# Value rows of the first batch: fetched by GpSimd's indirect DMAs instead of SyncE's loads

## The reference, cut to what matters

```python
query_sparse = relu(einsum('btd,nde->btne', x, enc_q))
value_sparse = relu(einsum('btd,nde->btne', x, enc_v))
idx, mask = _causal_window_indices(Tt, WINDOW)             # 64 rows back
dist = sqrt((diff * diff * m_h).sum(-1) + 1e-08)           # diff = key - query
neg_d, loc = top_k(-dist, 32)
infl = exp(-topd) / (exp(-topd).sum(-1) + 1e-08)
context = einsum('btk,btkd->btd', infl, v_h[batch_ix, top_idx])
out = (q_h * (context + gate * 0.1 * heb_ctx)) @ decoder
```

## Time and profile before

| | |
|---|---|
| median of 2 runs | 807.11 us (805.77 to 808.45) |
| the profiled execution's own time | 806.9 us, span 805.1 us |
| busy, share of the span | PE 88%, DVE 84%, POOL 53%, ACT 52% |
| busy share of the 16 DMA engines | 8.9% on SP's queue |
| mean granted clock of TensorE | 0.926 of full speed |

### The profile page before, as it was taken

The page is one execution under the profiler, slowest core; times in us unless marked ns, Lnnn a source line. Parts: engine busy times, 40 slices in busy tenths (PEclk is TensorE's granted clock), DMA queues, the critical chain, the costliest instruction groups (busy, mean ns, idle before and its releaser), DMA issues.

```text
span 805.1 us, 11834 instructions
## 1 busy us (share of the span) xinstructions
PE 708.7 (88%) x3368; PEld 504.3 (63%) x3368; DVE 678.5 (84%) x2785; ACT 416.6 (52%) x754; POOL 424.4 (53%) x504
## 2 busy tenths in 40 slices
PE   3979998998997999998997999999998899888833
PEld 2636765665665676665575667676766676667823
DVE  3876768769989999979879989976799999758894
ACT  2745353654766465464556464456674455466300
POOL 2265355564657654564655846564747656434131
PEclk9978999999989999999999999999999999995555
DMA  9920000000000000001000000001000000010000
GB/s 290 347 61 1 1 0 0 2 1 19 12 1 10 10 14 7 14 2 30 15 1 10 9 7 17 11 1 32 13 1 10 8 16 17 3 41 6 18 26 18
DMA packets 25697, 22.17 MB, mean 28 GB/s; under 512 B 1892, under 2 KB 23424, under 8 KB 25120
## 3 DMA queue, kind: packets, MB, share of 16 engines
q1 hardware_dynamic: 25632, 21.40, 8.9%
HBM read 19.17 MB, written 2.23 MB: 27 GB/s over the span
## 4 chain that ended last, share of the span: by engine, by line
DVE 49%; PE 35%; issue 5%; ACT 5%; DMA 4%; POOL 1%; SPq 0%; DVEq 0%; ACTq 0%
DVE S L790 12%; PE bank_G L505 9%; PE bank_X L505 9%; DVE Wk L1192 8%; PE bank_U L505 8%; PE bank_A L505 8%; DVE m L1189 6%; DVE Wk L798 5%; DMA vw<-vscratch 4%; DVE GWk L790 2%; DVE Wlo L790 2%; ACT L1261 2%; ACT Ed L1256 1%; DVE wT L790 1%; DVE La L790 1%
## 5 line engine op out<-in xcount | busy, mean ns | idle before, releaser
L505 PE MATMUL bank_A<-S,WdT 128*128 128x512 f32 x368 | 189.3, 614 | 11.6 <-DVE S L790 8.1
L1498 POOL TENSOR_TENSOR Wlo<-Wgu,Whi 128x256 fp32r<-128x256 f32 x138 | 111.1, 811 | 132.3 <-ACT Whi L1256 131.8
L1256 ACT ACTIVATE S<-bank_G 128x512 f32<-128x512 f32 x184 | 108.1, 595 | 124.0 <-PE bank_G L505 106.1
L1498 POOL TENSOR_TENSOR S<-S,Rb 128x512 f32<-128x512 f32 x88 | 120.2, 1367 | 78.1 <-DVE S L790 74.6
L790 DVE TENSOR_TENSOR S<-S,bank_U 128x512 f32<-128x512 f32 x184 | 123.6, 678 | 40.5 <-PE bank_U L505 28.7
L1256 ACT ACTIVATE Whi<-Wgu 128x256 fp32r<-128x256 f32 x184 | 74.4, 413 | 79.8 <-PE bank_U L505 76.4
L505 PE MATMUL bank_U<-xH,Whi 128*128 128x512 f32 x184 | 97.7, 531 | 6.2 <-DVE S L790 6.2
L505 PE MATMUL bank_G<-xH,Whi 128*128 128x512 f32 x184 | 100.7, 547 | 1.7 <-POOL Wlo L1498 1.6
L505 PEld LDWEIGHTS bank_A<-S,WdT 128*128 128x128 f32 x368 | 67.1, 194 | 50.2 <-issue 21.8
L790 DVE TENSOR_TENSOR S<-S,Rb 128x512 f32<-128x512 f32 x88 | 84.3, 959 | 2.6 <-ACT Rb L1256 0.6
L1192 DVE MATCH_REPLACE8 Wk<-m,Wk 128x79 f32<-128x79 f32 x384 | 81.7, 222 | 0.0
(11 more groups left out here) (232 smaller groups left out, 1444.8 us busy)
## 6 DMA issues: line engine op xcount, KB each, us to landing
vw<-vscratch SPq DMA_DIRECT2D x32, 158.0 KB
Wgu<-in_Wgu SPq DMA_DIRECT2D x2, 2048.0 KB, 15.3
xs<-in_x SPq DMA_DIRECT2D x4, 256.0 KB, 7.0
wqk<-in_w_qkv SPq DMA_DIRECT2D x1, 1024.0 KB, 7.5
Wgu<-in_Wgu SPq DMA_DIRECT2D x1, 1024.0 KB, 9.3
vscratch<-mo SPq DMA_DIRECT2D x4, 256.0 KB
out<-xs SPq DMA_DIRECT2D x3, 256.0 KB, 2.3
Wgu<-in_Wgu SPq DMA_DIRECT2D x1, 512.0 KB, 5.5
```

The costliest lines, as they stand in the source:

```text
L505: return engine.matmul(dst, lhsT, rhs, start=start, stop=stop)
L1256: return engine.activation(dst, src, f, bias=bias, scale=scale, accum_out=acc)
L1498: return engine.tensor_tensor(dst, a, b, op)
```

## The change

Only batch 0 changes its way of fetching. GpSimd writes a table `row_of` of 128 x 32 row numbers once (partition `p`, column `n` holds `16 n + p`). For each of the 8 groups it issues four indirect DMAs of 79 rows, one per tile, 32 in all, each of which reads its row numbers from a column of the table. They wait for the same things as the loads did: the stored value rows, and `ctx` of group `g - 2`. SP no longer issues the 8 loads of batch 0, and PE waits for all four fetches of a group. The batches 1 to 3 keep SP's loads. The table `ORDER` is new for PE, DVE, ACT and POOL over the whole program; its SP string differs in one place. The bodies of all other steps are the same.

```diff
@@ ORDER @@
     "sp":
-        "vvvvvvvvvsvvvvvvvvvsvvvvvvvvvsvvvvvvvssvvss",
+        "vvvvvvvvvsvvvvvvvvvsvvvvvvvvvsvvvvvvsvsvvss",
...
@@ program
+        U32 = mybir.dt.uint32
+        row_of = sb("row_of", [128, NG * GT], U32)
@@ values() of sync_engine
                     for g in range(NG):
                         yield
+                        if b == 0:
+                            continue
                         if g == 0:
                             sp.wait_ge(f"st_v{b}", 32)
                         if g >= 2:
                             sp.wait_ge(full(bank("ctx", b, g - 2)), nth("ctx", b, g - 2) + 1)
-                        elif b > 0:
+                        else:
                             sp.wait_ge(full(bank("ctx", b - 1, g + NG - 2)), nth("ctx", b - 1, g + NG - 2) + 1)
                         load(f"ld_v{g % 2}", vw[g % 2][:, :, :], windows(b, g))
@@ turns() of tensor_engine
-                    pe.wait_ge(f"ld_v{s}", 16 * (b * (NG // 2) + g // 2 + 1))
+                    if b:
+                        pe.wait_ge(f"ld_v{s}", 16 * ((b - 1) * (NG // 2) + g // 2 + 1))
+                    else:
+                        pe.wait_ge(f"ld_i{s}", 16 * GT * (g // 2 + 1))
@@ gpsimd_engine
+            def fetches():
+
+                yield
+                engine.iota(row_of[:, :], [[TQ, NG * GT]], base=0, channel_multiplier=1).then_inc(sems("row_of"), 1)
+                rows = vd[0]
+                for g in range(NG):
+                    for i in range(GT):
+                        yield
+                        po.wait_ge("row_of", 1)
+                        po.wait_ge("st_v0", 32)
+                        if g >= 2:
+                            po.wait_ge(full(bank("ctx", 0, g - 2)), nth("ctx", 0, g - 2) + 1)
+                        n = GT * g + i
+                        engine.indirect_dma_start(vw[g % 2][:, i, :], None, rows,
+                                                  bass.IndirectOffsetOnAxis(row_of[0:WK, n:n + 1], 0)).then_inc(
+                                                      sems(f"ld_i{g % 2}"), 16)
@@
-                  q=every(weights), p=every(adds))
+                  q=every(weights), p=every(adds), v=fetches())
```

More of the change, by code:

```diff
@@ L38 @@
     "sp":
-        "vvvvvvvvvsvvvvvvvvvsvvvvvvvvvsvvvvvvvssvvss",
+        "vvvvvvvvvsvvvvvvvvvsvvvvvvvvvsvvvvvvsvsvvss",
     "pe":
[L41 to L48, removed]
+        "yyeeyeeemeeeemaeeaeeeeeeeayasammmsmmaeemaesemsmeeeeeemmeeeemeeumemeeeumaemameaeeemeeaeeemuemummeeeye"
@@ new lines @@
+        "emmmymeeeeeemeeymeemeeemmemeeemeeememeeeeemmmyemeseeseesemseemeemeeeemmemyeemymeeheemeyeeemmeemeemee"
+        "emeeemeeeheeeehhmmhhmehhemmmeeemyheeeeededamdmaedaeeadaetmdatmamdmteetmeeeeedmmeemeemteeeemeeateaeea"
+        "emamtmmtsetseefeeemmfteeemmteeemmteeefeeefmfmeeteetmfemefeemfmeemsmseeeyeeteytemmthyeetemmteeememmet"
+        "meheeheememeeeehhmheheyheemammheeeeemdmdmaedaeemedaedamteeedteaeeaeteedtmmemmdmeeemteemeeeetmetmemee"
+        "aeemteeataeeaeemesemsmfmetfeetfteefefmefmtemtemeefmefmetmetsetsemeteetememeeeaeeetmmeahmmeemeeeeemee"
@@ L49 @@
+        "mheehemheheehamhhmmmeeememheaeeeedmdedmaemdeeameemeedteatdmeemdmeemmetemteeedemeammeeetemtatemaeeemm"
+        "eeeaeetefteefmmmtmeeeeeeetemtmmemmfeeeeteemteemmeeeetmtmtmmfhtftffthfhfhhfhfhhfffhfdfdddttddddtttttt"
         "tttttttttttt",
     "dve":
-        "yyyyyyyylyyyeycyeyeyyyyeyayeyylyyycayeyyeyymlmmyeayemyyaeaemaeaemeluemauelemuueeuumauueulemeuaemelem"
-        "eemeyyyyyyyylemeyyyemyeyyemlyyyyeyemeyyelememyeyyyemleemeyyemleeeemlehhemhhelemhhyyeyemyyyyyyleyyyem"
-        "yeyhyyyyheymehyyemhhhlyooeemoeaoaemoklkkkoekaemkkakakolkoekakgkkemgaekemkkaeemklekgemkkkekgkleaemagy"
@@ L54 @@
[L54 to L58, removed]
@@ L59 @@
-    "act":
[L60 to L65, removed]
@@ L66 @@
-    "pool":
[L67 to L70, removed]
+        "yyyyyyyyylyyyeycyeyyeyyeyyyyaeylayeceyyyylyyymmamyeemyyaaeemaeaelmeuueuemeluauuumuuueemeaelmeaemeelm"
@@ new lines @@
+        "eemeelmeyyyyyeemyelymyyyyeyyyeymyyeyeylmyeyemeyyyeymleemeemylyeeeelmyyhyhehehymeyelmhyhyyyeyyeyeymye"
+        "lmeyyyeymeyylyhemhehhhheemyoleoemoemoaokakkkokkkaklkeoaeaokkkgkamkaekekmegkelmkekaeekmgelmkkkkakeeag"
+        "ymkeygkylkeemkegkmyekyelmefkgkeefmkkelmekgkfekmekkfeleemgeelmyygyhyhyhyhyyegyeymeyyhyhylyeymyeygyhye"
+        "ymeelmehhyhheemheomleoaooaemokkkeokekoamlkkkekegaoekkakkkmlgkkaeemkeamegkkleamkgeekekkmkelmkgkaeekam"
+        "kelkekmefgekmgkfkkklfkeekmkgekkfegmelgemeegeelmageeamhhehhelmehhemelhemhheemhhelhemoeoemooeoakkkolek"
@@ new lines @@
+        "kmkkeaekmakgekokkoleakmakekegakkemekmlkegkekkgkmeklkeeameamekkgelkmfkkeegmeelmkkkkkegeemkkgleekmkgee"
+        "mkgfhhhhgfhhgfhfhhfhhhfooofkokkkkkookkokkogkkkgkkkkkkgkkkgkkkkkgkkkgkkkgkgkkkkkkgkgggg",
+    "act":
+        "xxyxyyxexeecxeecxxexexxxayaseesyxaeesxsexexexexexexaeexxuaeaxexexexexueuxeyexxexexexyxeexexexexexexe"
+        "xexexyesxexsesxexeyxexexesxmyexyxeexexexhxexeexexexexehxxhheehxhheexxyhexekkexnkxknnnkenkaxeannkgxka"
+        "nngxeexenxeaxexexexexenagxaexnegsxsexfxeeyxxegexexexfexefxgexexefxexesmsxeyexexgxygxeexexhexhexehxex"
+        "exexhhxyhhxeehexkkexenknknxknaxeenkaxkngnxekexexanngxexneexexeaxxgeenxenxaxegxeeaxxesxseefxegxfxfexg"
+        "eexexfexgsxeegxexsexexxxemeexexexhxexhexhehxxhaeehhxexeheaxkkxenkenxknnkenxkenxexengkxaknnxeexgxeanx"
+        "eexeaxexenganxxeexexexgefxexexexexgexfxeexgexeeegmgfhfhhfhhfhhfhkkfnnknknnknknngnnkknngnngnnggggg",
@@ L71 @@
+    "pool":
+        "vlllyyllllllmmamlaamaalamlamlllmallmlmlmllmmyylllmlmllmlmllmlmymlllmllmllmlyyllmlmllmlmlmllmyhovvvlm"
+        "vvvvvhllmholomooooqaomvvvvaaqaalplalvamqllvvmppvlmllamqllqmvvvvplvmpplvvvmllqmvvvlmlvplmqlmvvvvplplm"
+        "qlylmylplmppmlllmhollymlmlhlmholmooollooqalolplqaammmaalqpapmlamllaqplmmllqppmllmqlmlplqmllppmlqmpml"
+        "lplpllmlmlmllmhollmhlmholmloolmoaoqlomaampallaqoalalmqlpapmllmqplmqlmllmpplqmlmllqmlmplpmpmqppphohho"
+        "ooooqooqpppqqpqppqppqpqpp",
 }
```

## The result

The changed kernel takes 837.75 us (median of 2 runs, 836.08 to 839.42) against 807.11 us: 1.038 times the time, 95% interval 1.034 to 1.043, so 30.6 us slower. The forecast was 812 us with a range to 837. Slower by over 2% was the second most likely outcome of the text (0.27), and the size was outside its range.

The account below looks back on a forecast made before the run. It took PE and DVE, both about 92% busy from 196 to 360 us, as the bound, with POOL having room. Waits of 1.4 + 0.6 + 3.5 = 5.5 us on 806.9 us gave 812.4, forecast 812 us, range 802 to 837.

Parts of the forecast that it names:

- the fetches: 32 indirect DMAs on POOL, 196 to 360 us: 35.2 us of its 69.7 us idle, adding 5.5 us to the kernel.
- the order: New instruction order outside the fetches, whole program: put at 0, with 4 us to either side.
- the second rival: Fetches hold DVE as POOL's products do: 6.3 us more on DVE, 819 us in all; chance 0.10.
- The rival of the order: The new instruction order is worth more than the fetches cost: wins 5 us, 802 us; chance 0.13.
- The middle is 1.1 us: Time one fetch holds POOL, taken between its own products of 0.787 and 1.353 us.
- the slack of one turn of 4.1 us: PE's time per block, 4.1 us, by which a `Wlo` can come later without PE noticing.
- 26 t - 25.6: Added time for a fetch of t us (over 1.37): 26 fetches in groups of three and more, less slacks.
- the fetches' own waits for `ctx` of group g - 2: POOL's waits before other groups' fetches: its list is two or more blocks ahead, so nothing was put.
- The tight place: Group of four fetches behind the first `ctx`: POOL needs 10.25 us, PE 6.8, so PE stands still 3.5 us.
- SP's loads and the table of row numbers: Dropping SP's 8 loads gains nothing; one table instruction before POOL's first `Wlo`, in 9.35 us idle, costs nothing.
- The landing: A group's last fetch stands 8 us or more ahead of PE's matching `ctx`, against 3.8 us a window: nothing.
- The first rival: A fetch holds POOL for long, deciding from 1.6 us on: 833 us at 2.0, 880 at 3.8; chance 0.24.

## Why the prediction was wrong

Both terms that made up the forecast failed, and in opposite directions: the fetches, put at 5.5 us, cost 50, and the order, put at 0, gave back 20. The measured +30.6 us is what is left of the two.

**The order: "The new order everywhere else ... I put 0, and 4 us to either side."** It is -20 us. I had compared how far each batch's steps stand from the expert blocks, found them within a block, and taken that for equality. What a table can gain lies finer, perhaps in which POOL product runs beside which DVE instruction. I had the price of that in hand in the very rows that I used for the second rival, 17 us in this stretch alone, and used it only for what POOL's new work might add, not for what a new order might take away. The rival of the order had the right sign for this term, with 5 us and 0.13.

**The fetches, first their duration: "The middle is 1.1 us."** 1.91 us and a gap of 0.30 were measured, twice as much. The bounds, 0.22 and 3.8 us, held the value. Two elementwise products gave no reason for the middle; per row fetched the cost is 16.8 ns, which nothing in the trace before showed.

**The fetches, then the slack of one turn of 4.1 us.** This is the part of the mechanism that was wrong. The sum let groups of three or fewer cost nothing and gave each of the others 4.1 us. With the measured 2.21 us its formula, 26 t - 25.6, gives 31.9 us for the path, and measured are 50. That 806.9 + 31.9 = 838.8 us is nearly the time of the change is a coincidence of this error with that of the order. The formula fails for 16 fetches too: no place has more than two in a row, and they cost 17 us. Several things were wrong in it. It looked only for `Wlo` and `S` behind the fetches, and the longest single wait, 16.2 us, was DVE's for `hg`. And it gave the slack anew at every group, as if POOL had caught up in between. It also put nothing for the fetches' own waits for `ctx` of group g - 2; two of them waited, 1.07 us at 276 us and 6.13 us at 348 us, and what was queued behind waited too. The table of holds fits one stock of 15 to 20 us for the whole stretch. And it had no term for TensorE's clock, which fell with the waits (16 us between the same blocks). POOL's 69.7 us idle were no measure for it: 44.3 of them were waits for ACT and DVE, engines that themselves wait, by way of PE, for what POOL gives. That these come later when POOL does is the reading of this; no run isolates it.

**The tight place** was right in mechanism and size: 7.9 us by its working with the measured duration, 8.35 us in the profile.

**SP's loads and the table of row numbers**: right, nothing; `IOTA` takes 0.15 us at 0.8 us, in POOL's first idle time.

**The landing**: right in effect, wrong in size: 5.9 us, not under 3.8. No one waited.

**The first rival** (a fetch holds POOL for long, deciding from 1.6 us on) is the mechanism that came; its price at 2.0 us, 26 us, is too low for the same reason as the sum. **The second** (fetches hold DVE as POOL's products do, 6.3 us) came at most in part. The kernel to compare with is the one with the same order, in which this group takes 413 ns on average. Up to block 104 of the change:

```profile
L806 DVE SCALAR_TENSOR_TENSOR Wk<-Wk,Ed 128x79 f32<-128x79 f32 x32 | 15.1, 526 | 0.0
```

That is 3.6 us more in this group (15.1 against 11.5), and 2.0 us more of busy DVE over the whole program (644.6 against 642.6). Each of its instructions of over 1 us ends within 0.12 us of the end of a POOL product, none with a fetch. Two that lie wholly beside a fetch took 0.85 and 0.81 us instead of 0.23, and three one-input instructions beside fetches were longer by 0.5 to 0.7 us, so a fetch is not quite free for DVE, but these are five instructions in 32 fetches.

A fetch isn't stretched by DVE either: 1.94 us on average with DVE busy 4.9 of 20 us (200 to 220 us), and 1.92 us with DVE busy 19.5 of 20 us (300 to 320 us). The Trainium skill (DMA: Bandwidth & Descriptors, SWDGE vs HWDGE vs iDMA) has VectorE, in its two-port mode, locking GpSimd out of the memory in which the descriptor rings lie; no sign of that shows in these rows, which don't tell whether VectorE is in that mode here.

**The range** ended at 837, which the text calls t = 2.2 us; its own formula gives 838.6 us there. Had it been worked out right, 837.75 us would lie inside, by luck: two errors, of 45 and of 20 us, stood behind a sum of 5.5 us.

## What to carry to other kernels

When a change brings a new schedule, split it: the table without the new work is one run, and here it was worth -20 us under a change that cost +50. Don't take an engine's idle time for slack when the engines that it waits for wait for it in turn; take from it what a few dummy instructions show (here 15 to 20 of 70 us), not what the busy share leaves. Compare a row of the change with the kernel of the same order, not only with the one before. Try a load from SP with a partition count that is a multiple of 16, and use GpSimd's indirect DMAs only for addresses that aren't known.

## What the hardware showed that was not expected

- An indirect DMA of GpSimd holds it 1.91 us for 79 rows and 0.85 us for 16, plus a gap of 0.30 us before the next; a plain one of the same 79 rows 0.53 us. Landing after 5.9 and 2.0 us.
- A load of four windows from SP lands after 15.3 us with 79 partitions and 2.3 us with 80.
- DVE's busy time differs by 36 us between two orders of the same 2785 instructions, 26 us of it in two groups with two inputs in SBUF. One such instruction was booked as busy for 2.40 us instead of 0.23 and ended as the POOL product beside it did.
- PE's idle time of 38 us more came with 16 us more of busy time for the same work, at a granted clock of 0.90 instead of 0.98.
